# Values of two groups in one product of 256 columns, directly as tokens by features

## The chip, the cores and the metric

One core of a Trainium2 chip. The metric is the device time of one execution in microseconds (us). The engines are TensorE (PE; its weight loads are PEld), VectorE (DVE), ScalarE (ACT), GpSimd (POOL) and SyncE (SP), which here only issues transfers. Each takes its own instructions in order and waits on semaphores for the others.

## The reference

One block of a language model on 4 sequences of 512 tokens, 1024 features, all in fp32: an embedding (sum over 8 clipped shards, plus bias and positions), attention, and a small per-head MLP. The part that matters is the attention:

```python
qkv = q @ w_qkv.T                       # q: layernormed h, 4 x 512 x 1024
qs, ks, vs = jnp.split(qkv, np.cumsum(SPLITS)[:-1], axis=-1)
qh = qs.reshape(Bq, Sq, KVHEADS, G, HEAD_D)      # 8 groups of 4 query heads of 128
kh = ks.reshape(Bq, Sq, KVHEADS, HEAD_D)
vh = vs.reshape(Bq, Sq, KVHEADS, HEAD_D)
scores = jnp.einsum('bskgd,btkd->bkgst', qh, kh) * scale
scores = jnp.where(causal, scores, jnp.finfo(scores.dtype).min)
probs = jax.nn.softmax(scores, axis=-1)
attn = jnp.einsum('bkgst,btkd->bskgd', probs, vh)
return attn.reshape(Bq, Sq, NHEADS * HEAD_D) @ w_dense.T
```

## The kernel before

**Precision.** An fp32 operand is kept as two rounded halves, `_hi` (the value rounded) and `_lo` (the rest). `product` makes three matmuls of a product: hi by hi, hi by lo, lo by hi. The halves are made by ScalarE (a copy to the rounded type) and then VectorE (the difference), both reading PSUM.

**Units and steps.** The work goes in 32 units, one for each sequence b and group g; unit n = 8b + g. A unit's order is a string of steps written out by hand (FIRST for unit 0, STATS for g = 0 otherwise, MID, MLP0 and MLP for g = 1 to 4, GATHER, EMBED, TURN and LAST for g = 5, 6, 7; MID also where there is no MLP, and for unit 30), and `schedule` puts them in one list, `STEPS`. START stands before the first, REST after the last. Every engine walks through the same list and does its own part of each step. So the strings set the order on TensorE and the order on VectorE and ScalarE alike.

The steps of this case:
- `Q0` to `Q3`, `K`, `V`: projections of a group, features by tokens, 8 feature tiles x 3 matmuls with 512 columns into a bank of `fb` (two banks, taken in turn by all jobs). Q2 and Q3 are those of the own group; Q0, Q1, K and V those of the next. `D0` to `D7`: the output projection of the group before (4 heads x 3 matmuls each).
- `S0` to `S3`: scores of a head, in `sc`. `E`: their exponentials into `prob`, by ScalarE; it comes right behind S where the string has none. `N`: VectorE divides by the row sums (L964, L968) and sets `prob_ready`.
- `Ta`, `Tb`: ten transposes of `prob` into `tp` (L591), rounded by ScalarE (L835 to L841) and VectorE. `Ta` waits until all of `N` is done. `PV`: probabilities by values, in `pv`.
- `VT` (in FIRST `vt`, at the head of the unit): V lies in SBUF as `v_feat`, features by tokens, in the place of `prob`. Four transposes (L686) turn it to tokens by features, into `tp`; three of the four token tiles are split in v_hi and v_lo, the last is kept as fp32 in `v_last`.
- `H`, `Z`, `B`, `X`: transposes and products for other stages (`Z`: transposes of `hacc` for the statistics of the second norm).

The end of the string MID, of which EMBED is a variant:

```python
"S3 PV1 K N3 Q1 Ta3 PV2 Tb3 V PV3 VT"
```

STATS has `S3 Z3 PV1 Z4 K N3 Q1 Z5 Ta3 PV2 Z6 Tb3 V Z7 PV3 VT`, FIRST `S3 K N3 Q1 Ta3 PV2 Tb3 V PV3 VT`, and MLP `S3 P N3 PV1 o K U0 U1 Ta3 PV2 U2 U3 Q1 Tb3 V PV3 VT`.

**At the start.** Q0, K, Q1 and V of the first unit (`ALONE`) are made in banks of their own, in two halves of 256 columns each: steps a0 to a3 do the first half of the tokens while the second half is still being normalised and turned (`X4` to `X7`).

**Weights.** A tile is [128, 512]; Q, K and V have two, D has one. Its halves stand in one of RW = 11 places of `w_both`. In the first sequence (and again for the first tiles of the second) a raw tile comes to `w_raw` (RAW = 4 places), ScalarE rounds it (L805), GpSimd makes the low half (L1126), and SyncE stores both halves in DRAM; later they are fetched from there. Tile m takes the place of tile m - RW, once that one's step is done; `Tally` works out at which step (`splits`).

Of the kernel before, what the change touches and what calls it, by code (L numbers as in the profile page):

```python
# [6 lines left out]
F32 = mybir.dt.float32  # L7
# [21 lines left out]

RAW, RW = 4, 11  # L30

# [22 lines left out]

FIRST = ("S0 vt E0 N0 Q2 H0 Ta0 H1 S1 Tb0 H2 E1 N1 Q3 H3 Ta1 PV0 Tb1 H4 S2 H5 H6 H7 E2 N2 Q0 Ta2 PV1 Tb2 S3 K N3 Q1 Ta3 PV2 "
         "Tb3 V PV3 VT")
# [16 lines left out]
START = ("A G0 G1 G2 G3 w0 w1 w2 J0 J1 B0 B1 La0 B2 Lb0 B3 La1 J2 X0 X1 w3 Lb1 C0 B4 B5 La2 J3 X2 X3 Lb2 C1 w4 B6 B7 La3 "  # L73
         "X4 X5 Lb3 a0 C2 a1 X6 X7 C3 a2 a3 Q0 K Q1 V")
REST = "D0 D1 D2 Z0 D3 Z1 D4 Z2 D5 Z3 D6 Z4 D7 Z5 Z6 Z7 e0 e1 e2 Y0 Y1 e3"


def unit(order, b, g):

    n = 8 * b + g  # L80
    out = []
    for t in order.split():
        kind = t.rstrip("0123456789")
        i = int(t[len(kind):] or 0)
        pair = 2 * (g - 1)
        if kind in ("S", "E", "N", "Ta", "Tb", "PV", "d") or t in ("Q2", "Q3"):
            out.append(Step(kind, b, g, i))
            if kind == "S" and f"E{i}" not in order.split():
                out.append(Step("E", b, g, i))
        elif kind == "vt":  # L90
            out.append(Step("VT", b, g, 0))
        elif kind in ("Q", "K", "V", "VT"):
            out.append(Step(kind, (n + 1) // 8, (n + 1) % 8, i))
        elif kind == "D":
            out.append(Step(kind, (n - 1) // 8, (n - 1) % 8, i))
        elif kind == "H":
            out.append(Step(kind, b, 0, i))
        elif kind in ("A", "G", "J", "B", "C", "La", "Lb", "X", "a", "w"):
            out.append(Step(kind, b + 1, 0, i))
        elif kind in ("Z", "Y", "e"):  # L100
            out.append(Step(kind, b - 1, 0, i))
        elif kind == "W":
            out.append(Step(kind, b, 0, 0))
        elif kind in ("f", "p", "o"):
            out.append(Step(kind.upper(), b - 1, 0, pair))
        elif kind in ("F", "P"):
            out.append(Step(kind, b - 1, 0, pair + 1))
        elif kind == "q":
            if pair > 0 and b > 0:
                out.append(Step("O", b - 1, 0, pair - 1))  # L110
        elif kind == "u":
            out.append(Step("U", b - 1, 0, 4 * pair + i))
        elif kind == "U":
            out.append(Step("U", b - 1, 0, 4 * (pair + 1) + i))
    return out
# [33 lines left out]
def aside(s):  # L149
# [8 lines left out]
FIRST_SPLITS = [Step(k, 0, 0, i) for k, i in (  # L158
    ("B", 1), ("Lb", 0), ("X", 1), ("Lb", 1), ("X", 3), ("X", 4), ("X", 5), ("Lb", 3), ("X", 7), ("C", 3), ("Q", 0))]


class Tally:


    def __init__(self):
# [13 lines left out]
        for s in STEPS:  # L179
            if s.kind in ("Q", "K", "V"):  # L180
                which = {"Q": s.i, "K": HQ, "V": HQ + 1}[s.kind]
                own = [("qkv", 2 * ((HQ + 2) * s.g + which) + half) for half in range(2)]
            elif s.kind == "D":
                own = [("dense", 8 * s.g + s.i)]
            else:
                own = []
            if own:
                self.tile[s] = len(self.tiles)
            self.tiles += own
            user += [s] * len(own)  # L190

# [28 lines left out]
def tower_kernel(nc, x_cols, x_row, table, bias, pos, edge_cols, w_qkv, w_dense, w_mlp, perm_cols, out):  # L220
# [20 lines left out]
    def head(s):  # L241
        return 4 * (8 * s.b + s.g) + s.i

    def turn_a(s):

        return 9 * (8 * s.b + s.g) + {"VT": 0, "Ta": 1 + 2 * s.i, "Tb": 2 + 2 * s.i}[s.kind]

    def turn_b(s):
        return 5 * (8 * s.b + s.g) + {"VT": 0, "Ta": 1 + s.i}[s.kind]

    ctx = ExitStack()
    with ctx:
        def sb(name, shape, dt, at=ctx):
            return at.enter_context(nc.sbuf_tensor(name, shape, dt))
# [4 lines left out]
        def sem(name):  # L259
            return ctx.enter_context(nc.semaphore(name))  # L260
# [17 lines left out]
        k_lo = sb("k_lo", [P, S], F32R)  # L278
        v_hi = sb("v_hi", [P, TT - 1, D], F32R)
        v_lo = sb("v_lo", [P, TT - 1, D], F32R)  # L280

# [9 lines left out]
        pt_last = sb("pt_last", [P, 2, P], F32)  # L291
        v_last = sb("v_last", [P, D], F32)
        prob = sb("prob", [P, P_LEN], F32)
        v_feat = prob[:, 0:S]
        mlp_w = sb("mlp_w", [P, 2, S], F32)
# [73 lines left out]
        alone_free = sem("alone_free")  # L369
        v_alone_free = sem("v_alone_free")  # L370
        h_stats = sem("h_stats")
        h_moments = sem("h_moments")
# [181 lines left out]
        def _(pe):  # L554
            def product(dst, a_hi, a_lo, b_hi, b_lo, first, last):
                pe.matmul(dst, a_hi, b_hi, start=first, stop=False)  # L556
                pe.matmul(dst, a_hi, b_lo, start=False, stop=False)  # L557
                return pe.matmul(dst, a_lo, b_hi, start=False, stop=last)  # L558

            def projection(s, dst, t0, t1):  # L560
# [9 lines left out]
                return mm  # L570

            def scores(s):
                q = s.i % 2
# [19 lines left out]
            def values(s):  # L593
                r = s.i % 2

                pe.wait_ge(tpa_free, turn_a(Step("Tb", s.b, s.g, s.i)) + 1)
                if head(s) > 0:
                    pe.wait_ge(pv_free, head(s))
                if tally.sides[s] > 0:
                    pe.wait_ge(side_free, tally.sides[s])  # L600
                for j in range(TT - 1):
                    at = slice(PT_OFF[j], PT_OFF[j] + S - j * P)
                    product(pv[:, j * P:S], v_hi[:, j, :], v_lo[:, j, :], pt_hi[:, r, at], pt_lo[:, r, at],
                            j == 0, False)
                pe.matmul(pv[:, S - P:S], v_last[:, :], pt_last[:, r, :], start=False, stop=True).then_inc(pv_full, 1)  # L605

# [51 lines left out]
            for s in STEPS:  # L658
                if s.kind == "S":
                    scores(s)  # L660
                elif s.kind == "Ta":
                    pe.wait_ge(prob_ready, 4 * head(s) + 4)
                    pe.wait_ge(tpa_free, turn_a(s))
                    for t in range(TT):
                        mm = turn(0, t * P, t, 0)
                    mm.then_inc(tpa_full, 1)
                    pe.wait_ge(tpb_free, turn_b(s))
                    for t in range(1, TT):
# [6 lines left out]
                elif s.kind == "PV":  # L675
                    values(s)
                elif s.kind == "VT":
                    pe.wait_ge(*free(Step("V", s.b, s.g, 0)))
                    if turn_a(s) > 0:
                        pe.wait_ge(tpa_free, turn_a(s))  # L680
                        pe.wait_ge(tpb_free, turn_b(s))
                    else:
                        pe.wait_ge(*free(ALONE[1]))
                        pe.wait_ge(*free(ALONE[2]))
                    for j in range(TT):
                        mm = pe.transpose(tp[:, j // 2, (j % 2) * P:(j % 2 + 1) * P],  # L686
                                          v_feat[:, j * P:(j + 1) * P], ident[:, :])
                        if j == 1:
                            mm.then_inc(tpa_full, 1)
                    mm.then_inc(tpb_full, 1)  # L690
                elif s.kind in ("Q", "K", "V"):
                    if s.kind == "Q" and s.g == 0 and s.i == 0:
# [94 lines left out]
        def _(act):  # L787
# [35 lines left out]
            for s in STEPS:  # L823
# [29 lines left out]
                elif s.kind == "V":  # L853
                    act.wait_ge(*filled(s))
                    act.activation(v_feat, product_at(s), copy).then_inc(free(s)[0], 1)
                elif s.kind == "VT":
                    act.wait_ge(tpa_full, turn_a(s) + 1)
                    act.activation(v_hi[:, 0:2, :], tp[:, 0, 0:256].rearrange("p (j d) -> p j d", j=2), copy)\
                       .then_inc(tpa_hi, 1)
                    act.wait_ge(tpb_full, turn_b(s) + 1)  # L860
                    act.activation(v_hi[:, 2, :], tp[:, 1, 0:D], copy)
                    act.activation(v_last[:, :], tp[:, 1, D:2 * D], copy).then_inc(tpb_hi, 1)
                elif s.kind == "H":
# [61 lines left out]
        def _(dve):  # L925
# [21 lines left out]
            for s in STEPS:  # L947
# [51 lines left out]
                elif s.kind == "C" and s.i == 3:  # L999

                    dve.wait_ge(row_ready, 8)
                    for half in range(2):
                        dve.tensor_copy(h_tok[:, s.i, half * S:(half + 1) * S], first_bank(2 * s.i + half))\
                           .then_inc(last_free, 1)
                elif s.kind == "VT":
                    dve.wait_ge(tpa_hi, turn_a(s) + 1)
                    dve.tensor_tensor(v_lo[:, 0:2, :], tp[:, 0, 0:256].rearrange("p (j d) -> p j d", j=2),
                                      v_hi[:, 0:2, :], ALU.subtract).then_inc(tpa_free, 1)
                    dve.wait_ge(tpb_hi, turn_b(s) + 1)
                    dve.tensor_tensor(v_lo[:, 2, :], tp[:, 1, 0:D], v_hi[:, 2, :], ALU.subtract).then_inc(tpb_free, 1)  # L1010
                elif s.kind == "D":
# [218 lines left out]
```

## Time and profile before

| | |
|---|---|
| median of 3 runs | 2605.9 us (2605.78 to 2606.75) |
| the profiled execution | 2605.48 us, span 2603.7 us |
| TensorE matmuls, busy | 2586.4 us (99%), 12982 instructions |
| TensorE weight loads, busy | 2111.4 us (81%) |
| VectorE, ScalarE, GpSimd, busy | 1195.6 (46%), 989.9 (38%), 318.0 us (12%) |
| granted clock of TensorE, mean | 0.999 of full speed |
| transfers | 425.69 MB, 163 GB/s |

The span is from the first to the last instruction. A matmul's duration holds its way through the array, so matmuls that follow one another overlap, and what one costs is the distance from start to start. The timeline merges like instructions; the figure in brackets is idle time of the engine before it, with what ended it.

### The profile page before, as it was taken

What the parts mean: (1) busy time and instruction counts of PE and PEld (TensorE: products, weight loads), DVE (VectorE), ACT (ScalarE), POOL (GpSimd) and SP (SyncE); (2) the same over time, 40 slices, a digit from 0 to 9 for tenths busy, and PEclk for the clock granted to TensorE, in tenths of its full rate; (3) what the DMA queues carried; (4) which work ended last, traced back from release to release, by engine and by line L of the source; (5) the groups of instructions that cost most, each with busy time, mean ns of one, the idle gap of its engine ahead of it and who ended that gap; (6) DMA issues with size and microseconds to landing.
All of it is one profiled execution on the core that took longest, in us unless ns stands there. A gap on an engine that the chain in (4) does not pass through costs nothing.

```text
span 2603.7 us, 35197 instructions
## 1 busy us (share of the span) xinstructions
PE 2586.4 (99%) x12982; PEld 2111.4 (81%) x12982; DVE 1195.6 (46%) x3147; ACT 989.9 (38%) x2612; POOL 318.0 (12%) x266
## 2 busy tenths in 40 slices
PE   9999999999999999999999999999999999999998
PEld 7888888888877777888887877788888777778884
DVE  5444444554444434455453443445445344434444
ACT  5544444454343333324333334322433333332232
POOL 5233334333000000100000000010000000000002
PEclk9999999999999999999999999999999999999999
DMA  5456568655444434644443443463444444434432
GB/s 175 176 203 221 212 213 277 227 202 204 172 144 156 146 130 145 204 146 143 146 157 125 166 154 134 138 214 132 146 152 146 138 146 162 142 133 144 143 128 97
DMA packets 135191, 425.69 MB, mean 163 GB/s; under 512 B 15918, under 2 KB 15918, under 8 KB 135022
## 3 DMA queue, kind: packets, MB, share of 16 engines
q1 hardware_dynamic: 127488, 398.00, 43.9%
q0 software_dynamic: 7424, 25.17, 3.5%
q8 instruction: 106, 1.74, 0.3%
q14 instruction: 63, 0.52, 0.1%
q10 hardware_dynamic: 110, 0.26, 0.0%
HBM read 322.71 MB, written 100.66 MB: 163 GB/s over the span
## 4 chain that ended last, share of the span: by engine, by line
PE 98%; DMA 1%; DVE 1%; ACT 0%; issue 0%; ACTq 0%; POOLq 0%; POOL 0%; DVEq 0%
PE fb L556 22%; PE fb L558 22%; PE fb L557 22%; PE tp L591 6%; PE pv L556 3%; PE sc L556 3%; PE sc L557 3%; PE pv L558 3%; PE sc L558 3%; PE pv L557 3%; PE sc L643 2%; PE fb L652 2%; PE sc L582 1%; PE pv L605 1%; PE pv L637 1%; PE fb L637 1%
## 5 line engine op out<-in xcount | busy, mean ns | idle before, releaser
L556 PE MATMUL fb<-xn_hi,w_both 128*128 128x512 f32 x1504 | 596.1, 396 | 0.0
L558 PE MATMUL fb<-xn_hi,w_both 128*128 128x512 f32 x1504 | 587.5, 391 | 0.0
L557 PE MATMUL fb<-xn_lo,w_both 128*128 128x512 f32 x1504 | 586.1, 390 | 0.0
L556 PE MATMUL fb<-at_hi,w_both 128*128 128x512 f32 x992 | 394.8, 398 | 0.0
L558 PE MATMUL fb<-at_hi,w_both 128*128 128x512 f32 x992 | 387.7, 391 | 0.0
L557 PE MATMUL fb<-at_lo,w_both 128*128 128x512 f32 x992 | 386.8, 390 | 0.0
L829 ACT ACTIVATE prob<-sc,neg_max 128x128 f32<-128x128 f32 (+3 forms) x512 | 263.4, 527 | 287.1 <-DVE neg_max L960 287.0
L556 PEld LDWEIGHTS fb<-xn_hi,w_both 128*128 128x128 f32 x1504 | 282.5, 188 | 75.4 <-issue 18.8
L1015 DVE TENSOR_TENSOR hacc<-hacc,fb 128x512 f32<-128x512 f32 x256 | 176.0, 687 | 356.1 <-PE fb L558 355.7
L558 PEld LDWEIGHTS fb<-xn_hi,w_both 128*128 128x128 f32 x1504 | 282.3, 188 | 60.4
L557 PEld LDWEIGHTS fb<-xn_lo,w_both 128*128 128x128 f32 x1504 | 282.7, 188 | 57.0
L1126 POOL TENSOR_TENSOR w_both<-w_raw,w_both 128x512 fp32r<-128x512 f32 x180 | 230.0, 1293 | 416.3 <-ACT w_both L805 416.1
L957 DVE CUSTOM_DVE_ANT_0 sc<-sc,mask 128x128 f32<-128x128 f32 (+3 forms) x512 | 237.0, 520 | 4.1 <-PE sc L558 4.0
L985 DVE TENSOR_TENSOR at_lo<-pv,at_hi 128x512 fp32r<-128x512 f32 x124 | 85.6, 690 | 306.2 <-ACT at_hi L844 306.2
L556 PEld LDWEIGHTS fb<-at_hi,w_both 128*128 128x128 f32 x992 | 186.3, 188 | 46.0 <-issue 9.7
L558 PEld LDWEIGHTS fb<-at_hi,w_both 128*128 128x128 f32 x992 | 186.2, 188 | 40.0
L557 PEld LDWEIGHTS fb<-at_lo,w_both 128*128 128x128 f32 x992 | 186.6, 188 | 36.7
L990 DVE TENSOR_TENSOR q_lo<-fb,q_hi 128x384 fp32r<-128x384 f32 x126 | 70.3, 558 | 312.0 <-ACT q_hi L852 311.6
L968 DVE TENSOR_SCALAR prob<-prob,inv_sum 128x128 f32<-128x128 f32 (+3 forms) x512 | 185.9, 427 | 4.5
L591 PEld LDWEIGHTS tp<-ident,prob 128*128 128x128 f32 x1280 | 151.6, 140 | 43.8 <-issue 19.8
L591 PE MATMUL tp<-ident,prob 128*128 128x128 f32 x1280 | 182.9, 273 | 0.4 <-DVE pt_lo L972 0.4
L851 ACT ACTIVATE q_first<-fb 128x128 f32<-128x128 f32 x126 | 35.0, 278 | 382.9 <-PE fb L558 382.9
(211 smaller groups left out, 3468.4 us busy)
## 6 DMA issues: line engine op xcount, KB each, us to landing
w_both<-qkv_halves SPq DMA_DIRECT2D x268, 512.0 KB, 3.7
w_both<-dense_halves SPq DMA_DIRECT2D x192, 512.0 KB, 3.8
qkv_halves<-w_both SPq DMA_DIRECT2D x96, 512.0 KB, 3.9
dense_halves<-w_both SPq DMA_DIRECT2D x64, 512.0 KB, 3.3
w_raw<-in_w_qkv SPq DMA_DIRECT2D x116, 256.0 KB, 4.2
w_raw<-in_w_dense SPq DMA_DIRECT2D x64, 256.0 KB, 3.7
h_rows<-hacc SPq DMA_DIRECT2D x32, 256.0 KB, 2.3
h_tok<-in_pos SPq DMA_DIRECT2D x12, 512.0 KB, 8.0
```

Source lines behind the costliest of these rows:

```text
L556: pe.matmul(dst, a_hi, b_hi, start=first, stop=False)
L557: pe.matmul(dst, a_hi, b_lo, start=False, stop=False)
L558: return pe.matmul(dst, a_lo, b_hi, start=False, stop=last)
L591: return pe.transpose(tp[:, at, c:c + P], prob[:, P_OFF[t] + j * P:P_OFF[t] + (j + 1) * P], ident[:, :])
L637: mm = pe.transpose(dst[:, j * P:(j + 1) * P], blocks(j), ident[:, :])
L829: act.activation(prob[:, P_OFF[t]:P_OFF[t] + w], sc[:, at, c:c + w], ACT.Exp, bias=neg_max[:, t:t + 1], scale=SCALE, accum_out=row_sum[:, ...
L957: dve.tensor_tensor_reduce(one, one, mask[:, S - w:S], 1.0, LOWEST, ALU.add, ALU.max, row_max[:, t:t + 1]).then_inc(tile_max, 1)
L968: dve.tensor_scalar(at, at, inv_sum[:, t:t + 1], None, ALU.mult).then_inc(prob_ready, 1)
L985: dve.tensor_tensor(lo[:, s.i, :], pv[:, :], hi[:, s.i, :], ALU.subtract).then_inc(pv_free, 1)
L990: dve.tensor_tensor(lo, product_at(s)[:, at], hi, ALU.subtract).then_inc(free(s)[0], 1)
L1015: dve.tensor_tensor(hacc[:, s.i, :], hacc[:, s.i, :], fb[:, bank(s), :], ALU.add)\
L1126: pool.tensor_tensor(w_lo[:, m % RW, :], w_raw[:, raw[m] % RAW, :], w_hi[:, m % RW, :], ALU.subtract)\
```

## The change

The values of two groups are made together, as tokens by features: the normalised tokens are the stationary operand, 128 tokens of one feature tile at a time, and the weights of the two groups (256 columns) are the moving one. `V0` makes token tiles 0 and 1, `V1` tiles 2 and 3, each into one bank of `fb`, from four weight tiles that are laid out anew on the host. That is done in every other unit. In units with odd g, V becomes V0 and VT becomes V1; in those with even g, V and VT fall out and Q1 takes the place of V. The turned values (`v_feat`, VT) go, and V0 and V1 are both emptied in step V1. `v_hi`, `v_lo` and `v_last` hold two groups. RW is 10.

```diff
-RAW, RW = 4, 11
+RAW, RW = 4, 10
-FIRST = ("S0 vt E0 N0 Q2 H0 Ta0 ...
+FIRST = ("S0 N0 Q2 H0 Ta0 ...
 START = (...
-         "X4 X5 Lb3 a0 C2 a1 X6 X7 C3 a2 a3 Q0 K Q1 V")
+         "X4 X5 Lb3 a0 C2 a1 X6 X7 C3 a2 Q0 K Q1 V0 V1")
...
+    if g % 2:
+        order = order.replace(" V ", " V0 ").replace(" VT", " V1")
+    elif " VT" in order:
+        order = order.replace(" Q1 ", " ").replace(" V ", " Q1 ").replace(" VT", "")
...
+            elif s.kind == "V" and s.i == 0:
+
+                own = [("qkv", 2 * ((HQ + 2) * (s.g + j // 2) + HQ + 1) + j % 2) for j in range(4)]
+                last = s._replace(i=1)
+                self.tile[last] = len(self.tiles)
...
-            user += [s] * len(own)
+            user += [last] * len(own)
...
+    def values_now(s):
+
+        if s in ALONE:
+            return [s]
+        return [v for v in (s._replace(i=0), s) if v not in ALONE] if s.i else []
...
+            def two_values(s, dst):
+
+                for c in range(2):
+                    t = 2 * s.i + c
+                    for k in range(KT):
+                        m = tally.tile[s] + k // 2
+                        if c == 0 and k % 2 == 0:
+                            pe.wait_ge(*ready(m))
+                        w = slice(k % 2 * 2 * D, (k % 2 + 1) * 2 * D)
+                        mm = product(dst[:, 2 * D * c:2 * D * (c + 1)], xn_hi[:, k, t * P:(t + 1) * P],
+                                     xn_lo[:, k, t * P:(t + 1) * P], w_hi[:, m % RW, w], w_lo[:, m % RW, w],
+                                     k == 0, k == KT - 1)
+                return mm
...
+                if s.i == 0:
+                    pe.wait_ge(*free(Step("V", s.b, s.g - s.g % 2, 1)))
...
                 elif s.kind == "V":
-                    act.wait_ge(*filled(s))
-                    act.activation(v_feat, product_at(s), copy).then_inc(free(s)[0], 1)
-                elif s.kind == "VT":
...
+                    for v in values_now(s):
+                        act.wait_ge(*filled(v))
+                        two = product_at(v).rearrange("p (c g d) -> p g c d", c=2, g=2)
+                        if v.i == 0:
+                            act.activation(v_hi[:, :, 0:2, :], two, copy).then_inc(v_rounded, 1)
+                        else:
+                            act.activation(v_last[:, :, :], two[:, :, 1, :], copy)
+                            act.activation(v_hi[:, :, 2, :], two[:, :, 0, :], copy).then_inc(v_rounded, 1)
...
-                elif s.kind == "VT":
...
+                elif s.kind == "V":
+                    for v in values_now(s):
+                        dve.wait_ge(v_rounded, values_half(v) + 1)
+                        two = product_at(v).rearrange("p (c g d) -> p g c d", c=2, g=2)
+                        if v.i == 0:
+                            dve.tensor_tensor(v_lo[:, :, 0:2, :], two, v_hi[:, :, 0:2, :], ALU.subtract)\
+                               .then_inc(free(v)[0], 1)
+                        else:
+                            dve.tensor_tensor(v_lo[:, :, 2, :], two[:, :, 0, :], v_hi[:, :, 2, :], ALU.subtract)\
+                               .then_inc(free(v)[0], 1)
```

## Rows read from the trace of the kernel before

**Rows 1.** The page, busy time, TensorE's clock in 40 slices, and the chain

```profile
PE 2586.4 (99%) x12982; PEld 2111.4 (81%) x12982; DVE 1195.6 (46%) x3147; ACT 989.9 (38%) x2612; POOL 318.0 (12%) x266
...
PEclk9999999999999999999999999999999999999999
...
PE 98%; DMA 1%; DVE 1%; ACT 0%; issue 0%; ACTq 0%; POOLq 0%; POOL 0%; DVEq 0%
```

**Rows 2.** Waits of TensorE: releaser, us in total, times, longest us

```profile
PE tp L591 <- DVE pt_lo L972: 0.4, 1, 0.4
```

**Rows 3.** Timeline of TensorE in unit 2: start us, duration, instruction, count

```profile
240.61 0.39 PE L556 MATMUL fb<-xn_hi,w_both 128*128 128x512 f32 x1
...
246.06 1.03 PE L591 MATMUL tp<-ident,prob 128*128 128x128 f32 x8
...
256.22 0.60 PE L686 MATMUL tp<-ident,prob 128*128 128x128 f32 x4
256.65 0.39 PE L582 MATMUL sc<-k_first,q_first 128*128 128x128 f32 x2
```

**Rows 4.** Groups of TensorE by line and form

```profile
L556 PE MATMUL fb<-xn_hi,w_both 128*128 128x512 f32 x1504 | 596.1, 396 | 0.0
...
L686 PE MATMUL tp<-ident,prob 128*128 128x128 f32 x128 | 19.2, 273 | 0.0
```

**Rows 5.** Timeline of VectorE in unit 2

```profile
241.61 0.69 DVE L990 TENSOR_TENSOR k_lo<-fb,k_hi 128x512 fp32r<-128x512 f32 x1 [2.30 <-ACT k_hi L849]
...
242.43 3.16 DVE L968 TENSOR_SCALAR prob<-prob,inv_sum 128x128 f32<-128x128 f32 x4
```

**Rows 6.** Timelines of TensorE and VectorE in unit 0, head 0

```profile
59.73 0.44 PE L591 MATMUL tp<-ident,prob 128*128 128x128 f32 x2
...
58.40 1.27 DVE L968 TENSOR_SCALAR prob<-prob,inv_sum 128x128 f32<-128x128 f32 x4
```

**Rows 7.** Timeline of TensorE at the start, first and last of 97 in a row

```profile
37.00 0.28 PE L556 MATMUL pv<-xn_hi,w_both 128*128 128x256 f32 x1
...
48.52 0.28 PE L556 MATMUL pv<-xn_hi,w_both 128*128 128x256 f32 x1
```

**Rows 8.** Timeline of TensorE, 256-column products in `values`, two places

```profile
255.63 0.29 PE L556 MATMUL pv<-pt_hi,v_hi 128*128 128x256 f32 x1
...
256.00 0.38 PE L605 MATMUL pv<-pt_last,v_last 128*128 128x128 f32 x2
...
700.65 0.28 PE L556 MATMUL pv<-pt_hi,v_hi 128*128 128x256 f32 x1
...
701.00 0.39 PE L605 MATMUL pv<-pt_last,v_last 128*128 128x128 f32 x2
```

**Rows 9.** Timeline of ScalarE in unit 2

```profile
237.89 0.21 ACT L829 ACTIVATION_READ_ACCUMULATOR prob<-sc,neg_max 128x1 f32 x1
...
240.99 0.59 ACT L849 ACTIVATE k_hi<-fb 128x512 fp32r<-128x512 f32 x1
```

**Rows 10.** Timeline of GpSimd in unit 2

```profile
242.17 2.54 POOL L1126 TENSOR_TENSOR w_both<-w_raw,w_both 128x512 fp32r<-128x512 f32 x2 [6.90 <-ACT w_both L805]
```

**Rows 11.** Timeline of TensorE in unit 8 (STATS) and unit 14 (EMBED)

```profile
692.66 0.39 PE L556 MATMUL fb<-xn_hi,w_both 128*128 128x512 f32 x1
...
698.10 0.60 PE L637 MATMUL fb<-ident,hacc 128*128 128x128 f32 x4
...
1181.39 0.39 PE L556 MATMUL fb<-xn_hi,w_both 128*128 128x512 f32 x1
```

**Rows 12.** Timeline of VectorE in units 8 and 14

```profile
694.47 1.28 DVE L968 TENSOR_SCALAR prob<-prob,inv_sum 128x128 f32<-128x128 f32 x4
...
1183.20 1.28 DVE L968 TENSOR_SCALAR prob<-prob,inv_sum 128x128 f32<-128x128 f32 x4
```

**Rows 13.** L707, the program's first matmuls: ns min/median/max; then the timeline

```profile
L707 PE MATMUL sc<-mask,ones x8: 592/1061/1193, 2.5 to 23.2; 128*128 128x512 f32 x8
...
2.47 5.46 PE L707 MATMUL sc<-mask,ones 128*128 128x512 f32 x6 [2.47 <-POOL ident L1121]
```

More of the change, by code:

```diff
@@ L41 @@
 Step = namedtuple("Step", "kind b g i")
-FIRST = ("S0 vt E0 N0 Q2 H0 Ta0 H1 S1 Tb0 H2 E1 N1 Q3 H3 Ta1 PV0 Tb1 H4 S2 H5 H6 H7 E2 N2 Q0 Ta2 PV1 Tb2 S3 K N3 Q1 Ta3 PV2 "
+FIRST = ("S0 N0 Q2 H0 Ta0 H1 S1 Tb0 H2 E1 N1 Q3 H3 Ta1 PV0 Tb1 H4 S2 H5 H6 H7 E2 N2 Q0 Ta2 PV1 Tb2 S3 K N3 Q1 Ta3 PV2 "
          "Tb3 V PV3 VT")
@@ L89, in unit @@
                 out.append(Step("E", b, g, i))
-        elif kind == "vt":
-            out.append(Step("VT", b, g, 0))
-        elif kind in ("Q", "K", "V", "VT"):
+        elif kind in ("Q", "K", "V"):
             out.append(Step(kind, (n + 1) // 8, (n + 1) % 8, i))
@@ L158 @@
 FIRST_SPLITS = [Step(k, 0, 0, i) for k, i in (
-    ("B", 1), ("Lb", 0), ("X", 1), ("Lb", 1), ("X", 3), ("X", 4), ("X", 5), ("Lb", 3), ("X", 7), ("C", 3), ("Q", 0))]
+    ("B", 1), ("Lb", 0), ("X", 1), ("Lb", 1), ("X", 3), ("X", 4), ("X", 5), ("Lb", 3), ("X", 7), ("C", 3))]
 class Tally:
@@ L179, in __init__ @@
         for s in STEPS:
-            if s.kind in ("Q", "K", "V"):
-                which = {"Q": s.i, "K": HQ, "V": HQ + 1}[s.kind]
+            last = s
+            if s.kind in ("Q", "K"):
+                which = {"Q": s.i, "K": HQ}[s.kind]
                 own = [("qkv", 2 * ((HQ + 2) * s.g + which) + half) for half in range(2)]
+            elif s.kind == "V" and s.i == 0:
+                own = [("qkv", 2 * ((HQ + 2) * (s.g + j // 2) + HQ + 1) + j % 2) for j in range(4)]
+                last = s._replace(i=1)
+                self.tile[last] = len(self.tiles)
             elif s.kind == "D":
@@ L244, in turn_a, with values_half @@
     def turn_a(s):
-        return 9 * (8 * s.b + s.g) + {"VT": 0, "Ta": 1 + 2 * s.i, "Tb": 2 + 2 * s.i}[s.kind]
+        return 8 * (8 * s.b + s.g) + {"Ta": 2 * s.i, "Tb": 2 * s.i + 1}[s.kind]
     def turn_b(s):
-        return 5 * (8 * s.b + s.g) + {"VT": 0, "Ta": 1 + s.i}[s.kind]
+        return head(s)
+    def values_half(s):
+        return 8 * s.b + s.g + s.i
+    def values_now(s):
+        if s in ALONE:
+            return [s]
+        return [v for v in (s._replace(i=0), s) if v not in ALONE] if s.i else []
     ctx = ExitStack()
@@ L278, in tower_kernel @@
         k_lo = sb("k_lo", [P, S], F32R)
-        v_hi = sb("v_hi", [P, TT - 1, D], F32R)
-        v_lo = sb("v_lo", [P, TT - 1, D], F32R)
+        v_hi = sb("v_hi", [P, 2, TT - 1, D], F32R)
+        v_lo = sb("v_lo", [P, 2, TT - 1, D], F32R)
         with ExitStack() as own:
@@ L291, in tower_kernel @@
         pt_last = sb("pt_last", [P, 2, P], F32)
-        v_last = sb("v_last", [P, D], F32)
+        v_last = sb("v_last", [P, 2, D], F32)
         prob = sb("prob", [P, P_LEN], F32)
-        v_feat = prob[:, 0:S]
         mlp_w = sb("mlp_w", [P, 2, S], F32)
@@ L370, in tower_kernel @@
         v_alone_free = sem("v_alone_free")
+        v_rounded = sem("v_rounded")
         h_stats = sem("h_stats")
@@ L602, in values @@
                     at = slice(PT_OFF[j], PT_OFF[j] + S - j * P)
-                    product(pv[:, j * P:S], v_hi[:, j, :], v_lo[:, j, :], pt_hi[:, r, at], pt_lo[:, r, at],
+                    product(pv[:, j * P:S], v_hi[:, s.g % 2, j, :], v_lo[:, s.g % 2, j, :], pt_hi[:, r, at], pt_lo[:, r, at],
                             j == 0, False)
-                pe.matmul(pv[:, S - P:S], v_last[:, :], pt_last[:, r, :], start=False, stop=True).then_inc(pv_full, 1)
+                pe.matmul(pv[:, S - P:S], v_last[:, s.g % 2, :], pt_last[:, r, :], start=False, stop=True).then_inc(pv_full, 1)
             def start_job(s):
@@ L662, in _ @@
                     pe.wait_ge(prob_ready, 4 * head(s) + 4)
-                    pe.wait_ge(tpa_free, turn_a(s))
+                    if head(s) > 0:
+                        pe.wait_ge(tpa_free, turn_a(s))
+                    else:
+                        pe.wait_ge(*free(ALONE[1]))
+                        pe.wait_ge(*free(ALONE[2]))
                     for t in range(TT):
@@ L666, in _ @@
                     mm.then_inc(tpa_full, 1)
-                    pe.wait_ge(tpb_free, turn_b(s))
+                    if head(s) > 0:
+                        pe.wait_ge(tpb_free, turn_b(s))
                     for t in range(1, TT):
@@ L676, in _ @@
                     values(s)
-                elif s.kind == "VT":
[L678 to L681, printed above, removed]
-                    else:
[L683 to L691, printed above, removed]
+                elif s.kind == "V":
+                    if s in ALONE:
+                        pe.wait_ge(first_free, 6)
+                        two_values(s, product_at(s)).then_inc(alone_full, 1)
+                    else:
+                        two_values(s, start_job(s)).then_inc(job_full, 1)
+                elif s.kind in ("Q", "K"):
                     if s.kind == "Q" and s.g == 0 and s.i == 0:
@@ L853, in _ @@
                 elif s.kind == "V":
-                    act.wait_ge(*filled(s))
-                    act.activation(v_feat, product_at(s), copy).then_inc(free(s)[0], 1)
-                elif s.kind == "VT":
[L857 to L862, printed above, removed]
+                    for v in values_now(s):
[6 more added lines that the diff above has]
+                            act.activation(v_hi[:, :, 2, :], two[:, :, 0, :], copy).then_inc(v_rounded, 1)
                 elif s.kind == "H":
@@ L1004, in _ @@
                            .then_inc(last_free, 1)
[L1005 to L1010, printed above, removed]
+                elif s.kind == "V":
+                    for v in values_now(s):
[4 more added lines that the diff above has]
+                               .then_inc(free(v)[0], 1)
+                        else:
+                            dve.tensor_tensor(v_lo[:, :, 2, :], two[:, :, 0, :], v_hi[:, :, 2, :], ALU.subtract)\
+                               .then_inc(free(v)[0], 1)
                 elif s.kind == "D":
@@ L1203 @@
         order += [g * HQ + i for i in range(HQ)] + [G * HQ + g, G * HQ + G + g]
-    w_qkv = w[order].reshape(-1, 2, 4, P, D).transpose(0, 1, 3, 2, 4).reshape(-1, P, 4 * D)
+    w_qkv = w[order].reshape(-1, 2, 4, P, D).transpose(0, 1, 3, 2, 4).reshape(G, HQ + 2, 2, P, 4 * D)
+    v = w[G * (HQ + 1):].reshape(G // 2, 2, 4, 2, P, D).transpose(0, 2, 4, 3, 1, 5).reshape(G, 2, P, 4 * D)
+    w_qkv[:, HQ + 1] = v
+    w_qkv = w_qkv.reshape(-1, P, 4 * D)
     w_dense = np.asarray(L0_attn_w_dense).reshape(KT, P, G, HQ, D).transpose(2, 0, 4, 3, 1)\
```

## The prediction

> **What bounds the kernel now.** I read the page first. TensorE is busy 99% of the span, at full clock, and it is 98% of the chain that ended last [rows 1]. So no other engine's saving counts unless it lets TensorE start something earlier, and every microsecond that TensorE stands still is a microsecond of the result. Then the waits of TensorE: the rows of that view add up to about 8 us, the longest of them the first matmul's 2.47 [rows 13], and those of the attention are singles below 1 us, as [rows 2]. The busy shares say nothing about how close the other engines come to making it wait. For that one needs the timeline of one group's unit, which I read for TensorE, VectorE, ScalarE and GpSimd side by side. From start to start, a product of 24 matmuls of 512 columns takes 246.06 - 240.61 = 5.45 us (0.227 us each) [rows 3]. The mean duration in the groups by form, 396 ns, is not its price, since matmuls overlap [rows 4]. What matters below is the softmax of head 3: its normalised rows are ready 0.47 us before the transposes `Ta3` that read them (242.43 + 3.16 = 245.59 against 246.06) [rows 3, 5]. That is all the slack there is, while TensorE runs `Q1`, 5.45 us of work, in between.
>
> **Turned values go.** `VT` is four transposes, 0.43 us between its start and the next instruction's [rows 3]; the 128 instructions are 32 such steps [rows 4]. They lie on TensorE between two other fp32 instructions and nothing waits on them: 32 x 0.43 = 13.8 us off. In the first unit this is not a saving. There the chain is the softmax of head 0: `Ta0` starts 0.06 us after its rows are ready (58.40 + 1.27 = 59.67, start 59.73) [rows 6], so taking a step out in front of it only makes TensorE wait. The new order also gives ScalarE four weight roundings there instead of some few, but the raw halves will have landed by then. I count this unit at nothing: -13.4 us.
>
> **Values as tokens by features.** A pair of groups had 2 x 24 matmuls of 512 columns and gets 2 x 48 of 256. The columns are the same, the number of matmuls doubles. The kernel already has 256-column products on these tiles, at its start: 96 of them lie between 37.00 and 48.52, 0.120 us each [rows 7]. A step is then 48 x 0.120 = 5.76 us instead of 5.45. Of 32 steps the first was already in 256s, so 31 x 0.31 = +9.6 us. Three 256-column matmuls of another product take 0.35 us (0.117 each) in one place and 0.37 (0.123) in another [rows 8]; these are the bounds, 31 x (5.62 - 5.45) = +5 and 31 x (5.90 - 5.45) = +14. I keep 0.120, as same shape and same tiles, though the operands change sides.
>
> The Trainium skill (TensorE: Matmul & The Clock Gate, Back-to-back issue gap) gives columns / 2.4 plus 2.5 ns for an isolated gap, so 109 ns for 256 columns and 216 for 512. By that estimate the step would grow by only 24 x 2.5 = 0.06 us, 1.9 us in all. The trace has about 13 ns above the columns' own time in each matmul, at 512 and at 256 alike, and it decides.
>
> **What the new order uncovers.** In units with odd group, `V` becomes `V0` and `VT` becomes `V1`; in even ones `V` and `VT` go and `Q1` moves from before `Ta3` to the place of `V`, after `Tb3`. So in FIRST, MID, EMBED and STATS the even units now read `K N3 Ta3` (STATS with `Z5` before `Ta3`). VectorE takes steps in this order: `N3`, the normalisation, is queued behind the rounding rest of `K`, and that needs K's last matmul. The exponentials of head 3 are done at 238.1, long before, but VectorE waits until ScalarE has rounded K (from 240.99), subtracts at 241.61, and normalises from 242.43 to 245.59 [rows 5, 9]. K's last matmul gives way to `Q1` at 240.61 [rows 3]. With `Q1` gone TensorE stands from 240.61 until 245.59 + 0.06 (the latency of [rows 6]) = 5.04 us. Behind the waiting `Ta3` are `PV2`, `Tb3`, `Q1`: nothing of it can pass, as TensorE takes its steps in order.
>
> Two prices, for the normalisation takes 3.16 us where GpSimd computes weight halves at the same time (242.17 for 2.54 us) [rows 10] and 1.28 where it does not:
> - first sequence (weights still split), units 0, 2, 4, 6: 4 x 5.04 = 20.2 us. The four show the same distance in the trace, 4.97 to 4.98 us before the latency. GpSimd's two tiles belong to K's step in either order, so I keep the 3.16; without that contention each would be 1.9 less, 7.5 in all, the lower bound.
> - units 14 and 22 (EMBED) and 30 (MID): K ends at 1181.39, rows ready 1183.20 + 1.28 = 1184.48: 3.15 us with the latency, three times 9.5 [rows 11, 12].
> - units 8, 16, 24 (STATS): 692.66 to 694.47 + 1.28, 3.15 as well, less the four transposes of `Z5` that still stand in between (from 698.10, four of them, 0.44): 3 x 2.71 = 8.1 [rows 11, 12].
> - the MLP units 10, 12, 18, 20, 26, 28 have `N3` ahead of `PV1` and K, and stay free; the odd units keep `Q1` in its place.
>
> Sum of the stalls: 37.8 us.
>
> **The rest at nothing.** Ten places: a tile is fetched when the one ten before it is used up, which is still over 20 us of matmuls ahead in every order (the four values tiles come free together, and the next that wants their places is the third tile of `D`, behind `S0 Q2 D0 D1 S1 Q3`), against landings of some 4 us. V0's bank is held until V1's step: ScalarE and VectorE empty it after `PV3`, under V1's 5.76 us; if not, `Q2` would wait. Four roundings in a row after V1 (4 x 0.6 us) lie ahead of head 0's exponentials, in the time in which VectorE looks for the maxima; head 0 has over 2.5 us of slack outside the first unit. The start loses the half product `a3` as cover for `X7`, but `a2`, 2.9 us, still lies between, and the two roundings take 0.59 and 0.69 [rows 5, 9]; the a3 in the trace starts at 37.00 [rows 7], where `Q0` now would. One extra step change per pair between fp32 and rounded matmuls costs nothing: the first matmul is later by 0.08 and the fp32 pair in front is shorter by as much.
>
> **The clock.** The page grants the full clock throughout [rows 1], but the first matmuls run at half of it, 1.2 GHz for 2.4: up to 1193 ns where the same form takes 592, and six of them take 5.46 us, so some 2.7 us lost, after 2.47 us in which the engine had not worked [rows 13]. Pauses in mid-kernel were below 1 us so far, so the trace does not say what a pause of 5 us does. From nothing to 2.7 us for each of the four long pauses: 0 to 11 us. I take 2.
>
> The Trainium skill (TensorE: Matmul & The Clock Gate, Why this matters for your kernels) warns that idle gaps between bursts of matmuls can send the array back to 1.2 GHz. By that rule each of the long pauses may end cold; it speaks against this change, and no row of this trace tests it.
>
> **Sum.** -13.4 + 9.6 + 37.8 + 2 = +36.0 us on the profiled execution's 2605.5 us (span 2603.7 and 1.8 around it), 0.4 below the median of the runs shown: 2641.5; I say 2641.
>
> **Rivals.**
> - Stalls as above, clock stays full, V at 0.117: 2605.5 - 13.4 + 5 + 37.8 = 2635; without GpSimd's contention 2628. Chance of this milder case 0.22.
> - The clock falls in most of the 5-us pauses and some of the 3-us ones: up to 10 x 2.7 on top of 2639.5; I expect 2645 to 2655. For it: the half-speed start. Against: these pauses are short and end in dense work. Chance 0.2.
> - The other side: no stall at `Ta3`. It needs `N3` to run before K ends. The exponentials end 2.5 us before K does and the four multiplications need 1.3 to 3.2, so the data would allow it: it decides whether VectorE really sits behind K's rounding. If it did not, the time would be 2605.5 - 13.4 + 9.6 = 2601.7, faster by 0.16%, or 2597 at the lower price of V. The trace speaks against: VectorE's order in [rows 5] is k_lo, then prob, in every unit of these orders. Chance 0.04.
> - The forecast itself: 0.54.
>
> Range: 2630 to 2654 takes the forecast, most of the milder case and most of the cold one. By over 0.2% (5.2 us, about what a measurement of this kernel can tell from no change): slower 0.96, within 0.02, faster 0.02.
>
> **What would show it.** The waits of TensorE should have a new first row, `tp` at the transposes of prob from VectorE's normalisation, ten times, 5.0 us at most, some 38 us. Value matmuls of 128x256 on fb, 1536 less those of the start, 0.120 us apart. L686's group gone. No wait on weights. Matmuls right after the long pauses show by their duration whether the clock fell. I am wrong if VectorE's normalisation stands ahead of k_lo, if 256-column value matmuls are more than 0.125 apart, or if TensorE waits on w_both or on fb's banks.

## The result, and the profile after

The changed kernel takes 2654.19 us (median of 4 runs, 2649.76 to 2658.88) against 2606.18 us before: ratio 1.0185, 95% interval 1.0172 to 1.0197. That is 48 us slower. The forecast was 2641 and its range ended at 2654.0, so the time lies just outside.

The run that was profiled is the fastest of the four: 2649.76 us, span 2648.0, 44.3 us more than before. The page of after, busy time and the chain; what answers to [rows 1]:

```profile
PE 2593.6 (98%) x13598; PEld 2144.3 (81%) x13598; DVE 1198.7 (45%) x3115; ACT 970.8 (37%) x2532; POOL 317.9 (12%) x266
...
PE 97%; DVE 2%; ACT 1%; issue 0%; DMA 0%; SPq 0%; POOLq 0%; POOL 0%; ACTq 0%; DVEq 0%
```

The busy shares hardly move, and yet VectorE now has 2% of the chain for 1%: its work is the same, but TensorE waits for it. The waits of TensorE name it (engine, releaser, us in total, times, longest):

```profile
PE tp L624 <- DVE prob L999: 35.8, 10, 4.8
PE sc L739 <- POOL ident L1156: 2.5, 1, 2.5
PE sc L777 <- DVE edges L975: 2.3, 1, 2.3
...
PE tp L624 <- DVE pt_lo L1003: 0.4, 1, 0.4
```

Ten waits at `Ta3` for the normalised rows, as forecast. There is no wait on a weight tile or on a bank of V. The view counts from the modelled end of the last matmul; from the moment at which `Q1` used to start, the ten come to 37.4 us. The timelines of after in unit 2, TensorE and then VectorE, against [rows 3, 5]:

```profile
252.91 0.39 PE L577 MATMUL fb<-xn_hi,w_both 128*128 128x512 f32 x1
258.11 1.97 PE L624 MATMUL tp<-ident,prob 128*128 128x128 f32 x8 [4.81 <-DVE prob L999]
...
260.73 0.63 PE L577 MATMUL pv<-pt_hi,v_lo 128*128 128x512 f32 x1
...
262.10 0.39 PE L640 MATMUL pv<-pt_last,v_last 128*128 128x128 f32 x2
```

```profile
254.13 0.69 DVE L1021 TENSOR_TENSOR k_lo<-fb,k_hi 128x512 fp32r<-128x512 f32 x1 [2.30 <-ACT k_hi L881]
254.74 0.17 DVE L995 RECIPROCAL inv_sum<-row_sum 128x4 f32<-128x4 f32 x1
254.94 3.11 DVE L999 TENSOR_SCALAR prob<-prob,inv_sum 128x128 f32<-128x128 f32 x4
```

K's last matmul starts at 252.91. 0.23 us later TensorE could take the next instruction, but it starts none until 258.11. And the eight transposes then last 1.97 us, where they took 1.03 in [rows 3]; a 512-column matmul behind them takes 0.63 for 0.39. The granted clock says why. In stretches of 1 us around another such place, unit 22, the columns are the stretch, its length, the busy time (instructions) of PE, PEld, DVE, ACT and POOL, TensorE's clock, DMA share and GB/s:

```profile
1865.00:1866.00 1.00, 0.05 (x1) 0.06 (x1) 0.89 (x3) 0.00 (x0) 0.00 (x0) 0.78 1.02 401
1866.00:1867.00 1.00, 1.00 (x5) 1.00 (x6) 0.00 (x0) 0.00 (x0) 0.00 (x0) 0.50 0.81 328
1867.00:1868.00 1.00, 1.00 (x6) 1.00 (x5) 0.28 (x1) 0.65 (x2) 0.00 (x0) 0.50 0.01 4
1868.00:1869.00 1.00, 1.00 (x4) 0.71 (x4) 0.78 (x2) 0.61 (x2) 0.00 (x0) 0.51 0.00 0
1869.00:1870.00 1.00, 1.00 (x9) 1.00 (x8) 0.20 (x1) 0.00 (x0) 0.00 (x0) 1.00 0.00 0
```

After a pause of 3.14 us TensorE works for some 3 us at 0.50, its lower level of 1.2 GHz. In this execution that follows six of the ten pauses: all four of 5 us, and those of units 22 and 30. From the start of Ta3 to PV2's last instruction these take 4.10, 3.99, 3.80, 4.41, 3.92 and 3.89 us, where it is 2.46 to 2.51 without a fall: 9.2 us lost.

The values, at the start of the program, V0 and then V1:

```profile
46.49 0.28 PE L575 MATMUL pv<-w_both,xn_hi 128*128 128x256 f32 x1
...
52.25 0.28 PE L575 MATMUL fb<-w_both,xn_hi 128*128 128x256 f32 x1
...
58.01 0.39 PE L615 MATMUL sc<-k_first,q_first 128*128 128x128 f32 x2
```

48 matmuls in 5.76 us, twice: 0.120 each, as in [rows 7].

**Where the 44.3 us are.** The pauses 37.4. The lower clock behind them 9.2. The start of the program 0.8: the first `S0` comes at 58.01 for 51.41, 6.60 later, of which V1 is 5.76. In this execution TensorE waited 2.3 us for VectorE's `edges`, and as that wait ended the granted clock went to 0.50 again, from 8.7 to 12.1 us, which no other kept trace shows there. The rest is 44.3 - 37.4 - 9.2 - 0.8 = -3.1, against -3.8 in the forecast (13.4 off, 9.6 on). Followed further, from Ta3 to the last matmul of PV3 and against the version with the normalisation first (below), the ten places lose 9.7 us instead of 9.2, which makes the rest -3.6. It can be seen alone in a pair of units without a pause: from first `S0` to first `S0`, units 10 and 11 took 83.09 us each before and 77.17 and 88.73 after, 0.27 less for the pair.

### The profile page after: what moved, and what is told of

It is laid out like the page before. It is cut to its first block, busy times and chain, and to the rows that moved or that the text cites. A ratio compares the mean times of both kernels' runs of the same rounds, so it can differ in the third digit from the quotient of the medians.

```text
span 2648.0 us, 36312 instructions
## 1 busy us (share of the span) xinstructions
PE 2593.6 (98%) x13598; PEld 2144.3 (81%) x13598; DVE 1198.7 (45%) x3115; ACT 970.8 (37%) x2532; POOL 317.9 (12%) x266
## 4 chain that ended last, share of the span: by engine, by line
PE 97%; DVE 2%; ACT 1%; issue 0%; DMA 0%; SPq 0%; POOLq 0%; POOL 0%; ACTq 0%; DVEq 0%
PE fb L575 22%; PE fb L577 22%; PE fb L576 22%; PE tp L624 6%; PE pv L575 3%; PE pv L577 3%; PE pv L576 3%; PE sc L575 3%; PE sc L577 3%; PE sc L576 3%; PE sc L678 2%; PE fb L687 2%; PE sc L615 1%; PE pv L640 1%; DVE prob L999 1%; PE pv L672 1%
## 5 line engine op out<-in xcount | busy, mean ns | idle before, releaser
L575 PE MATMUL fb<-xn_hi,w_both 128*128 128x512 f32 x1256 | 498.0, 397 | 0.0
L577 PE MATMUL fb<-xn_hi,w_both 128*128 128x512 f32 x1256 | 490.6, 391 | 0.0
L576 PE MATMUL fb<-xn_lo,w_both 128*128 128x512 f32 x1256 | 489.3, 390 | 0.0
L575 PEld LDWEIGHTS fb<-xn_hi,w_both 128*128 128x128 f32 x1256 | 235.9, 188 | 61.5 <-issue 14.3
L577 PEld LDWEIGHTS fb<-xn_hi,w_both 128*128 128x128 f32 x1256 | 235.7, 188 | 51.1
L576 PEld LDWEIGHTS fb<-xn_lo,w_both 128*128 128x128 f32 x1256 | 236.1, 188 | 47.8
L624 PE MATMUL tp<-ident,prob 128*128 128x128 f32 x1280 | 188.1, 279 | 36.3 <-DVE prob L999 35.8
```

Of the source, the lines that this page charges most:

```text
L624: return pe.transpose(tp[:, at, c:c + P], prob[:, P_OFF[t] + j * P:P_OFF[t] + (j + 1) * P], ident[:, :])
```

## The experiments

Each was timed beside the kernel before on the same chip. For the normalisation first, the work in the pauses, Q1 back and the control with ten places, the kernel before took 2606.61 us (21 runs). For the short pauses, GpSimd and the other control it took 2606.32 us (15 runs).

**The normalisation first.** One edit in `unit`, behind the replacements of the change:

```diff
+    if g % 2 == 0:
+        order = order.replace(" PV1 K N3 ", " N3 PV1 K ").replace(" PV1 Z4 K N3 ", " N3 PV1 Z4 K ")
+        order = order.replace(" S3 K N3 ", " S3 N3 K ")
```

> The changed kernel, but in the units with even group the normalisation N3 stands before PV1 and K (in FIRST before K) on VectorE, so that it no longer sits behind K's rounding. Theory (the whole loss is TensorE standing before Ta3, plus the clock that falls in it): the ten waits go but for some 1 us in unit 0, the clock stays at 0.999, and what is left is the gain without the four transposes, less the dearer products: 2606.2 - 13.4 + 9.6 + 1 = 2603.4 us, within 2601 to 2605. Rival (256-column values, bank V0 held long, or ten places cost something too): above 2608. Rival (VectorE's remaining work moves the wait elsewhere, PV1's rest delayed before PV2): waits on pv, some 2610 or more.

Measured: 2601.87 us (11 runs, 2601.43 to 2602.52), ratio 0.9983, interval 0.9974 to 0.9992, clock 0.999. In the view of TensorE's waits no row on `prob` is left. In unit 0 a little remains: `Ta3` starts 0.36 us after K's last matmul, for 0.23 elsewhere. VectorE in unit 2 (timeline):

```profile
243.51 1.27 DVE L1002 TENSOR_SCALAR prob<-prob,inv_sum 128x128 f32<-128x128 f32 x4
244.70 0.68 DVE L1019 TENSOR_TENSOR at_lo<-pv,at_hi 128x512 fp32r<-128x512 f32 x1
246.78 0.69 DVE L1024 TENSOR_TENSOR k_lo<-fb,k_hi 128x512 fp32r<-128x512 f32 x1 [1.40 <-ACT k_hi L884]
```

The rows are ready at 244.8, before `Ta3` at 245.79, and the four multiplications take 1.27 us: here they run before GpSimd's low halves. So all 52 us between this version and the changed kernel hang on one step's place in VectorE's order. What is left is the change's own gain, 4.7 us, where the sum without pauses said 3.8. Part of the difference is in unit 0, which the forecast counted at nothing: `Ta0` comes 7.97 us after the first `S0`, where it took 8.32 before.

**Work in the pauses.** At `Ta` of head 3, in the ten units alone; `dst` is pv, or in unit 24 the next job's bank:

```diff
+                for n in range(5 if s.b == 0 else 3):
+                    pe.matmul(dst, ones[:, :], mask[:, :], start=True, stop=True)
```

> The changed kernel, with 128x512 fp32 matmuls of constants put into the ten pauses before Ta3 (5 in units of the first sequence, 3 in the others, 0.85 us each), into a bank that nothing reads: TensorE works through most of each pause, and Ta3 starts when it did. If the loss beyond the waits is the clock falling in the pauses, the clock is back at 0.999, the four runs' spread goes, and the time is 2606.2 - 3.8 + 37.4 = 2639.8 us (2638 to 2642). Rival (the slow stretch after a pause has another cause, transfers or semaphores): above 2648 as before, with half-speed matmuls still there.

Measured: 2641.15 us (4 runs, 2640.42 to 2641.71), ratio 1.0132, interval 1.0117 to 1.0148. The timeline of TensorE in unit 2, then a stretch of 11 us around it in this kernel, then the same stretch in the changed one:

```profile
251.45 4.45 PE L704 MATMUL pv<-mask,ones 128*128 128x512 f32 x10
256.42 1.09 PE L624 MATMUL tp<-ident,prob 128*128 128x128 f32 x8 [0.52 <-DVE prob L1015]
```

```profile
252.00:263.00 11.00, 10.48 (x47) 7.24 (x46) 6.07 (x10) 3.47 (x8) 2.49 (x2) 1.00 0.41 145
```

```profile
252.00:263.00 11.00, 6.19 (x29) 5.28 (x28) 5.13 (x8) 3.53 (x8) 2.48 (x2) 0.84 0.41 145
```

`Ta3` still comes only after the same normalisation, but TensorE is at work meanwhile, the clock stays, and the transposes take 1.09 us. Doing more work makes the kernel 13 us faster (2654.19 - 2641.15), and the four runs lie within 1.3 us where they lay within 9.1. The 1.3 us above the expected 2639.8 are nearly all in one place: in unit 24 the filler itself waits 1.1 us for a bank that VectorE has to empty. The clock's share is thus 13 to 15 us in the median: 13.0 by this difference, and 14.9 if the 37.4 us of pauses are added to the 2601.87 of the version without them. The rival, that transfers or semaphores slow the stretch behind a pause, falls: the transfers are the same in the two stretches (share 0.41), TensorE still waits for the same normalisation, and no half-speed matmul is left.

**Q1 back in its place.** In even units V and VT are dropped and Q1 stays before Ta3, so nothing stands between Tb3 and PV3:

```diff
-        order = order.replace(" Q1 ", " ").replace(" V ", " Q1 ").replace(" VT", "")
+        order = order.replace(" V ", " ").replace(" VT", "")
```

> The changed kernel with Q1 back between K and Ta3 in the even units, so that nothing stands between Tb3 and PV3. Theory: Ta3 has its 0.47 us of slack again, and the cover is now missing before PV3, which must wait for the rounding of Tb3's tile behind PV2's: in the trace of before that ends about 1.7 us after Tb3. 16 units x 1.7 = 27 us: 2602.4 + 27 = 2629 us (2618 to 2634), no fall of the clock in so short pauses. Rival (only Ta3 needed the cover): 2602 to 2604.

Measured: 2628.06 us (4 runs, 2627.87 to 2628.23), ratio 1.0083, interval 1.0067 to 1.0098. The first row of TensorE's waits:

```profile
PE pv L575 <- DVE pt_lo L1011: 23.3, 16, 1.5
```

Sixteen waits of 1.3 to 1.5 us, and the clock stays at 0.999. With V gone from every other unit there is one product fewer to run while the other engines work, and two places need one. With nothing in front of PV3 there are 16 short pauses, with nothing in front of Ta3 ten longer ones.

**The short pauses alone.** The first edit with `if b == 0 and g % 2 == 0:`.

> The changed kernel with N3 ahead only in the first sequence's even units. The four 5-us pauses go, the six of about 3 us stay (3.14 three times, 2.70 three times = 17.5 us). If the clock also falls in some of the short pauses, as the trace of after shows for two of six, the runs scatter and lie above the sum: 2601.9 + 17.5 = 2619.4 without a fall, some 1.5 us for each that falls, median 2621 to 2624, clock 0.998 or less. Rival (only the long pauses cost clock): 2619.4 within 1 us, a narrow spread and clock 0.999.

Measured: 2624.87 us (5 runs: 2622.53, 2624.55, 2624.87, 2628.45, 2630.36), ratio 1.0079, interval 1.0065 to 1.0093, clock 0.998 in the profiled one, the fastest. The median lies 5.5 us above the sum without a fall. In the profiled execution two of the six are followed by slow matmuls, one of them after the shorter kind of pause. TensorE's timeline at the other one and at a place that stays fast, then the clock behind the shorter pause:

```profile
1192.59 1.97 PE L627 MATMUL tp<-ident,prob 128*128 128x128 f32 x8 [2.98 <-DVE prob L1002]
1350.54 1.09 PE L627 MATMUL tp<-ident,prob 128*128 128x128 f32 x8 [2.54 <-DVE prob L1002]
```

```profile
700.00:703.00 3.00, 2.96 (x12) 2.67 (x13) 1.91 (x4) 1.26 (x3) 0.00 (x0) 0.57 0.30 117
```

(The pause before 700.04 is 2.54 us in the view's count, and the clock is at 0.57 behind it.) So short pauses cost clock as well, sometimes. That this is also the scatter between runs is read from their mean clocks, since only one execution of each kernel has a trace: 0.998, 0.997, 0.997, 0.995 and 0.995 for the five times above, and in the changed kernel 0.994, 0.993, 0.992, 0.990 for 2649.76, 2653.21, 2655.18, 2658.88.

**GpSimd out of the normalisation.** The weight tiles that take K's places are rounded after `Ta3`:

```diff
+            if [s.kind for s in STEPS[place:place + 3]] == ["K", "N", "Ta"]:
+                place += 2
```

> The changed kernel with the weight roundings that follow K put off until after Ta3, so that GpSimd makes no low halves while VectorE normalises. If GpSimd's work is what makes the normalisation 3.16 us for 1.28, the four pauses of the first sequence shrink by 1.9 to some 3.1 us, ten in all below 3.2: 7.5 us less standing, and fewer falls of the clock (each some 1.6 us): 2640 to 2647 us against 2654. Rival (the slow normalisation has another cause, such as ScalarE's copies or transfers): four pauses of 5 us as before and 2650 or more.

Measured: 2642.95 us (4 runs, 2640.24 to 2652.03), ratio 1.0149, interval 1.0131 to 1.0167. VectorE in unit 2, then TensorE, then the row of waits:

```profile
253.10 1.27 DVE L1001 TENSOR_SCALAR prob<-prob,inv_sum 128x128 f32<-128x128 f32 x4
```

```profile
254.43 1.09 PE L626 MATMUL tp<-ident,prob 128*128 128x128 f32 x8 [2.98 <-DVE prob L1001]
```

```profile
PE tp L626 <- DVE prob L1001: 28.5, 10, 3.0
```

The four multiplications take 1.27 us for 3.11, and the waits fall from 35.8 to 28.5, 7.3 against the 7.5 forecast. The edit moves ScalarE's roundings as well as GpSimd's low halves, but the trace of the kernel before tells the two apart. A multiplication of 128x512 takes 0.47 us beside ScalarE's roundings alone, no more than the 0.48 without them. One of 128x256 takes 1.39 us beside GpSimd's low halves and 0.35 without. It was GpSimd's work that slowed them.

The median is 11.2 us below the changed kernel's 2654.19, so some 4 us are not in the waits. In the profiled execution the clock fell behind five of the ten pauses: four of the first sequence, now of 3.1 us, and unit 14's.

**Controls.** The kernel before with ten places; the list of the steps at which the first weights are rounded has one entry for each place and loses its last:

```diff
-RAW, RW = 4, 11
+RAW, RW = 4, 10
...
-    ("B", 1), ... ("C", 3), ("Q", 0))]
+    ("B", 1), ... ("C", 3))]
```

> The kernel before with ten places for weight halves instead of eleven, nothing else. Theory: the fetches are tens of us ahead, no difference: 2606.2 within 1.5 us. Rival (ten places delay weights): waits on w_both and over 2610.

Measured: 2606.55 us (10 runs), ratio 1.0000, interval 0.9991 to 1.0009. The kernel before with the edit of the first experiment:

> The kernel before with N3 ahead in the even units and nothing else. Theory: Ta3 had 0.47 us to spare, so an earlier N3 gives TensorE nothing: 2606.4 within 1.5 us; the gain of the version with N3 ahead is then the change's own. Rival (N3's place was worth something by itself): below 2604.

Measured: 2606.63 us (10 runs), ratio 1.0001, interval 0.9992 to 1.0010. The places cost nothing, and the earlier normalisation alone gives nothing: it was not late, its cover was taken away.

## Why the prediction was right on the wait and wrong on the clock

- **The wait at Ta3** (37.8 us): right, in its place, its ten units and both its sizes; 37.4 in the profiled execution. Removing it removes the loss (the normalisation first).
- **GpSimd's part of it** (7.5 us): right, 7.3.
- **The clock** is the step that failed: "From nothing to 2.7 us for each of the four long pauses: 0 to 11 us. I take 2." It measured 9.2 us in the profiled execution and 13 to 15 in the median (work in the pauses). Of the 13 us between the forecast and the result, 11 to 13 are this term. Two things were wrong. All four long pauses were followed by the lower clock, each for 1.3 to 2.0 us of loss, where the 2 us taken are less than a single fall at its price of 2.7. And the pauses of 3 us were given nothing in the forecast, though they cost some 5.5 us in the median by themselves (the short pauses alone). The rival "The clock falls in most of the 5-us pauses and some of the 3-us ones", 2645 to 2655, is what happened, at the upper end of its span; it had a chance of 0.2, and the half-speed rows of the program's start [rows 13] were the nearest rows to the question. Its price per fall, 2.7, was too high, but it should have been the likeliest case. The Trainium skill (TensorE: Matmul & The Clock Gate, Why this matters for your kernels) warns that idle gaps between bursts of matmuls can send the array back to 1.2 GHz. The traces agree that it happens, with 0.50 granted after the pauses, and they show that it need not: behind 5 of 13 traced pauses of 3.1 us the clock stayed full.
- **The range** ended at 2654.0, for it held that rival's time in part only.
- **Values by 256 columns** (+9.6) and **the transposes** (-13.4): 0.120 us a matmul measured; together -3.8 forecast, -4.7 in the version without pauses. The Trainium skill (TensorE: Matmul & The Clock Gate, Back-to-back issue gap) gives 109 ns for 256 columns as an isolated gap; no product of 256 columns in these traces is as close as that.
- **The rest at nothing**: ten places (control), V0's bank and the four roundings in a row (no wait on them): right. Unit 0 gained 0.35 us instead of nothing. The profiled execution's start was 0.8 us later than V1 accounts for, with a wait of 2.3 us on `edges`, which the change does not touch; the traces of the other versions show 0.9 us or less there. Their first `S0` comes at 56.83 to 57.97 us, so the start varies by about as much.

## What to carry to other kernels

When a step is taken out of an order, ask what it covered, and for each engine what stands queued in front of the work that the bound engine will wait for: here the data for the softmax were ready 2.5 us early, and the whole loss was one step standing behind another on VectorE. Price a pause of TensorE in mid-kernel above its length: these ten cost 37 us standing and 13 to 15 us of lower clock. If the order cannot be mended, matmuls of constants in the pause give that second part back; mending the order gave all of it, and the version with the normalisation first beats both kernels (2601.87 us, 0.17% below before).

## What the runs showed of the hardware

A pause of TensorE, in a kernel that keeps it busy 98% of the time, can be followed by some 3 us or more at the lower clock (0.50 granted), and the longer the pause, the more often. Over the traces of the changed kernel, the short pauses and GpSimd out of the normalisation, with the pause counted from the moment at which the next instruction could have started:

| pause | followed by the lower clock |
|---|---|
| 5.0 us | 4 of 4 |
| 3.1 us | 8 of 13 |
| 2.7 us | 1 of 9 |
| 1.3 to 1.5 us (Q1 back, by the view's count) | 0 of 16 |

One such fall cost 1.3 to 2.9 us, from the start of Ta3 to the last matmul of PV3 and against the version with the normalisation first. Pauses of the same length in the same program fall or not, and by the runs' mean clocks this differs from run to run: the runs of such a kernel scatter over 8 to 12 us, those of the others over 0.4 to 3.2.

VectorE's normalisation of 128x256 elements took 1.39 us while GpSimd subtracted 128x512 tiles, and 0.35 otherwise; ScalarE's rounding of 128x512 tiles beside it made no difference.
